# Due-time offsets for the engines' orders, and the down product's last chunk once a unit

## What is computed

```python
x = x + attn_a(layernorm(x))    # stage a: 8 heads of 64, low-rank keys and values, softmax over all 512
x = x + ffn(layernorm(x))       # stage f, two layers deep
x = x + attn_b(layernorm(x))    # stage b: 16 heads of 16, causal, score = dot^2 / (|q|^2 + |k|^2 - 2 dot + eps)
x = x + ffn(layernorm(x))       # stage f again, the same weights

def _layer(x, ...):             # one of the two layers of ffn
    q, k, v = split(shift_token(x) @ wqkv)          # 8 heads of 64, l2norm, rotary
    x = x + local_attention(q, k, v) @ wo           # window of 128 and the one before it
    h = layernorm(shift_token(x)) * lg + lb
    a, g = split(h @ w1 + b1)                       # 2 x 682 hidden features
    return x + (a * gelu(g)) @ w2 + b2              # the down product: 682 -> 256
```

## Time and profile before

| | us |
|---|---|
| median of 3 runs | 4440.92 |
| lowest, highest | 4433.65, 4452.77 |
| the profiled execution | 4441.2 |
| its span, first to last instruction | 4439.1 |
| TensorE busy with matmuls | 4132.5 (93%) |
| VectorE busy | 3291.9 (74%) |
| ScalarE busy | 2541.6 (57%) |
| GpSimd busy | 1674.8 (38%) |

### The profile page before, as it was taken

The page is one execution under the profiler, slowest core; times in us unless marked ns, Lnnn a source line. Parts: engine busy times, 40 slices in busy tenths (PEclk is TensorE's granted clock), DMA queues, the critical chain, the costliest instruction groups (busy, mean ns, idle before and its releaser), DMA issues.

```text
span 4439.1 us, 65596 instructions
## 1 busy us (share of the span) xinstructions
PE 4132.5 (93%) x23120; PEld 2596.3 (58%) x23120; DVE 3291.9 (74%) x7689; ACT 2541.6 (57%) x5480; POOL 1674.8 (38%) x1816
## 2 busy tenths in 40 slices
PE   8999989999999999987888877888999999999997
PEld 4665556666666666655555555555566666666664
DVE  5667677777767766659899999988677776677663
ACT  4555554445445445439888998876444454454441
POOL 2222355545545555430001001013565464465541
PEclk9999999999999999998889998988999999999998
DMA  2000000000001000000000001101000000100000
GB/s 79 10 16 6 24 11 6 3 3 4 24 8 30 15 8 8 26 19 20 20 21 22 22 18 28 37 18 34 3 6 3 3 25 8 32 17 17 13 20 22
DMA packets 63093, 78.57 MB, mean 18 GB/s; under 512 B 15344, under 2 KB 47392, under 8 KB 62768
## 3 DMA queue, kind: packets, MB, share of 16 engines
q1 hardware_dynamic: 62768, 74.39, 6.0%
HBM read 36.63 MB, written 12.58 MB: 11 GB/s over the span
## 4 chain that ended last, share of the span: by engine, by line
PE 65%; DVE 21%; issue 6%; ACT 5%; POOL 2%; DMA 0%; SPq 0%; POOLq 0%; DVEq 0%; ACTq 0%
PE wide L865 45%; PE o_ps L865 8%; PE wide L868 6%; PE turn_ps L868 5%; DVE x L1287 2%; DVE w_up L1387 2%; DVE turned L1338 2%; DVE prob L1399 1%; DVE w_up L1381 1%; DVE x L1393 1%; PE turn_ps L865 1%; DVE prob L1410 1%; POOL prob L1602 1%; ACT prob L1243 1%; DVE hid L1393 1%
## 5 line engine op out<-in xcount | busy, mean ns | idle before, releaser
L865 PE MATMUL wide<-x,w_up 128*128 128x512 f32 (+3 forms) x2528 | 843.0, 545 | 4.2 <-DVE x L1490 2.4
L865 PE MATMUL wide<-w_in,x_t 128*128 128x512 f32 (+2 forms) x1920 | 813.4, 568 | 17.5 <-ACT q_t L1164 8.1
L1602 POOL TENSOR_SCALAR prob<-prob,st 128x256 f32<-128x256 f32 (+1 forms) x1024 | 501.5, 508 | 758.8 <-DVE st L1423 756.4
L1223 ACT ACTIVATE prob<-prob,st 128x256 f32<-128x256 f32 (+1 forms) x1024 | 479.2, 471 | 259.9 <-DVE st L1410 259.5
L865 PEld LDWEIGHTS wide<-w_in,x_t 128*128 128x128 f32 x1920 | 342.2, 192 | 369.4 <-issue 360.6
L865 PEld LDWEIGHTS wide<-x,w_up 128*128 128x128 f32 (+2 forms) x2528 | 371.5, 195 | 289.5 <-issue 275.8
L865 PE MATMUL o_ps<-pt,v 128*32 128x128 f32 (+2 forms) x5120 | 500.0, 340 | 20.5 <-DVE pt L1439 9.9
L1575 POOL TENSOR_TENSOR sines<-raw,rot 128x512 f32<-128x512 f32 x256 | 354.0, 1403 | 331.2 <-ACT raw L1152 331.1
L1583 POOL TENSOR_TENSOR rn<-ss,minus_half 128x16 f32<-128x16 f32 x128 | 423.8, 3311 | 105.5 <-DVE ss L1333 98.7
L865 PEld LDWEIGHTS o_ps<-pt,v 128*64 128x64 f32 (+1 forms) x5120 | 322.1, 131 | 234.3 <-issue 145.6
L1254 ACT ACTIVATE o_t<-o_ps 128x512 f32<-128x512 f32 x192 | 114.2, 595 | 493.3 <-PE o_ps L865 493.3
(11 more groups left out here) (161 smaller groups left out, 7472.7 us busy)
## 6 DMA issues: line engine op xcount, KB each, us to landing
kept<-resid SPq DMA_DIRECT2D x16, 512.0 KB, 2.9
x<-kept SPq DMA_DIRECT2D x16, 512.0 KB, 3.3
w_up<-hid SPq DMA_DIRECT2D x62, 128.0 KB, 2.2
x<-hid SPq DMA_DIRECT2D x62, 128.0 KB, 2.4
shifted<-resid SPq DMA_DIRECT2D x32, 224.0 KB
w_in<-in_f_wqkv SPq DMA_DIRECT2D x4, 1536.0 KB, 6.5
w_up<-in_f_w SPq DMA_DIRECT2D x4, 1492.0 KB, 6.4
resid<-in_x SPq DMA_DIRECT2D x8, 512.0 KB, 8.9
```

The source lines that it names most:

```text
L865: return eng.matmul(out, lhsT, rhs, start=start, stop=stop, skip_group_check=True)
L1223: last = eng.activation(pr[:, local_span(t)], pr[:, local_span(t)], ACT.Exp, bias=sm[:, t:t + 1], scale=-1.0, accum_out=sm[:, 4 + t:5 + t])
L1602: last = eng.tensor_scalar(pr[:, local_span(t)], pr[:, local_span(t)], sm[:, 8 + t:9 + t], 1.0, ALU.mult, ALU.mult)
```

## The change

It has four pieces. `put` adds an offset from a new table, `DUE`, to a part's due time, by stage and kind; the table has 49 entries, for each of the three stages, between -0.284 and +0.31 units. `PATIENCE` goes from 0.3 to 0.321. The planned costs of the four `down` parts go from 2.3, 2.9, 2.3, 2.9 to 2.3, 2.3, 2.3, 3.4. And the 42-row products of all four tiles are issued behind the last tile's large ones, where they stood two by two behind the second and the fourth; since groups of two tiles in one bank are then open together, only tiles 0 and 2 start theirs with the start flag.

```diff
@@ cost
     if kind == "down":
-        return 2.9 if i % 2 else 2.3
+        return 3.4 if i == TILES - 1 else 2.3
@@ new
+DUE = {
+    ("f", "ss"): 0.022, ("f", "exp"): -0.039, ("f", "xt"): 0.015, ("f", "proj"): -0.076, ("f", "pt_a"): 0.074, ("f", "wt"): 0.161,
+    ("f", "raw"): 0.001, ("f", "pt_b"): -0.215, ("f", "rn"): -0.052, ("f", "nrm_h"): 0.11, ("f", "up_h"): -0.159, ("f", "inv"): 0.138,
+    ("f", "spread"): 0.092, ("f", "qk"): -0.021, ("f", "xt_c"): 0.102, ("f", "cos"): 0.073, ("f", "bn_f"): -0.014, ("f", "mix"): -0.114,
+    ("f", "res2"): 0.019, ("f", "join"): 0.004, ("f", "v_c"): -0.076,
+    ("a", "inv"): 0.001, ("a", "nrm_h"): -0.112, ("a", "ak_c"): -0.027, ("a", "pt_a"): 0.005, ("a", "aq"): 0.049, ("a", "mix"): 0.129,
+    ("a", "exp"): 0.061, ("a", "low"): 0.009, ("a", "xt_c"): 0.035,
+    ("b", "olog"): -0.057, ("b", "bqkv"): 0.046, ("b", "dup_b"): -0.232, ("b", "bn_h"): 0.31, ("b", "xt_c"): -0.017, ("b", "dup_a"): -0.272,
+    ("b", "bnum"): -0.044, ("b", "xt"): 0.053, ("b", "sel"): -0.065, ("b", "res"): -0.132, ("b", "brow"): -0.027, ("b", "turn_b"): -0.027,
+    ("b", "bclose"): -0.004, ("b", "bsq"): -0.284, ("b", "bss"): -0.066, ("b", "mix"): 0.123, ("b", "row"): -0.118, ("b", "bq"): 0.021,
+    ("b", "bden"): -0.001,
+}
@@ parts_of
     def put(kind, i, due, *follows):
-        out.append((kind, i, due, [f for f in follows if f is not None]))
+        out.append((kind, i, due + DUE.get((st, kind), 0.0), [f for f in follows if f is not None]))
@@ ordered
-PATIENCE = 0.3
+PATIENCE = 0.321
@@ the down product in tensor_program
                     for m in range(HC - 1):
-                        last = mm(ps[:, t * DIM:(t + 1) * DIM], hid[:, m, t * P:(t + 1) * P], w_down[:, m, :], m == 0, False)
-                    if i % 2:
-                        for t in DOWN_TILES[i - 1:i + 1]:
+                        last = mm(ps[:, t * DIM:(t + 1) * DIM], hid[:, m, t * P:(t + 1) * P], w_down[:, m, :], m == 0 and t % 2 == 0, False)
+                    if i == TILES - 1:
+                        for t in DOWN_TILES:
                             last = mm(ps[:, t * DIM:(t + 1) * DIM], hid[LAST_ROWS[t // 2], HC - 1, t * P:(t + 1) * P],
                                       w_down[LAST_ROWS[t // 2], HC - 1, :], False, True)
```

## The result

The changed kernel is slower. Its median is 4491.7 us (4 runs, 4485.9 to 4492.8), that of the kernel before beside it 4437.9 (4 runs, 4433.7 to 4452.8); the ratio is 1.0107, with a 95% interval of 1.008 to 1.0135. I had forecast 4402 and a range up to 4452. One execution of the kernel of experiment 9 took 4959.4 us at a granted clock of 0.84 and is left out of its ratio.

What follows compares the result with a forecast made beforehand. TensorE was taken to bound the feed-forward work and VectorE stage b. From 4441 us, 10.9 for the merged small products and 28 for the new order came off: 4402 us, range 4362 to 4452.

Steps and rivals of the forecast that it cites:

- Part 1: Down product: one block of small products per unit instead of two saves 0.35 us a unit, 10.9 us in all.
- part 2: The offsets and wider window change the engines' orders: 28 us gained, 16 at three edges and 12 in b.
- zero on the steady parts: Steady feed-forward units: the new order gains nothing, with under 0.6 us of 84 not busy on TensorE.
- only 6 us could be had there: Stage a: TensorE's idle time of 6.0 us, counted in the 108.9 us ceiling outside b.
- 6 us for changes of mode: Steady feed-forward units: one half-row block meeting more or less, about 0.2 us a unit, 6 us either way, range only.
- My own test in the last part: Steady feed-forward units: a change of over 1 us would mean the method was wrong about changes between full and half rows.
- minus 12 us: Stage b: the new order gives back a seventh of VectorE's 82.7 us idle time, 12 us.
- The third rival: Stage b: late clipping starves VectorE, 0.3 us a step over 192 steps, 58 us, so 4488 us; chance 0.12.
- the slack of 1.0 us a step: Stage b: the pair products' slack, TensorE's idle 197.6 us over 192 steps; delay beyond it makes VectorE wait.

Runs made afterwards that it cites:

- experiment 9: The changed kernel with added TensorE products in b, two ahead of pair products and two ahead of the transposes' wait: 4469.6 us, ratio 1.0031 to the kernel before.
- experiment 4: The kernel before with only the -0.004 offset of the closing product in b, small down products unmerged: 4469.5 us, ratio 1.0054.
- experiment 6: The merge of the small down products plus f's -0.021 offset for the query and key product, against the merge alone: 4459.3 us in one run.

## Why the prediction was wrong

**Part 1 was right.** 0.35 us a unit by the timeline was 0.36 in the profile, the eight small products took the 1.15 us worked out, and steady f units came to 83.4, where I had forecast 83.3, but only in the merge alone. The rule that a packed group costs one matmul and a few ns (the Trainium skill, "TensorE: Matmul & The Clock Gate", Measured speedup vs the span model) would have had no gain. The 0.36 us sides with the Trainium skill's page that has a change of mode drain the engine ("TensorEngine Tiling (Array Packing)", Key Properties).

**The step that failed is the sum for part 2.** I took TensorE's and VectorE's idle time as a ceiling, a share of it as the gain (28 us), and put zero on the steady parts, since a unit there is nearly all busy. Measured, part 2 was worth +62 us: the 51 between the spans and the 11 of the merge (by the table: -21 for a and the edge behind it, +36.5 and the merge's 11 for f, +35 for b). It has three terms, and I had the sign wrong in two and the place wrong in the third:

- *a*: the earlier trace rows show TensorE busy 434.0 of 440 us, so I wrote that only 6 us could be had there. The offsets took 2.1 us off each unit of 67, some 13 us over those 440 (an estimate, 6.5 units), twice that bound. A busy TensorE was not a full one: a transpose is shown as some 0.28 us long while the next starts 0.11 us after it, so gaps of up to some 0.16 us behind each group never appear as idle (an estimate, the difference of the two). In a steady unit of a, 396 matmuls before and after, the idle time shown fell from 1.0 to 0.35 us, a third of the 2.1. The count of matmuls in a stretch (2581, then 2632) shows what the busy share hides.
- *f*: zero, with 6 us for changes of mode. It was +1.5 us in each steady unit beside the merge's -0.35. A ceiling on gains says nothing on a loss, and in a it was no ceiling either. My own test in the last part (over 1 us in a steady unit) fired, though the cause was not the changes of mode that I named but one exposed wait of 1.65 us.
- *b*: minus 12 us, measured +35.

**The third rival had the start of the mechanism right, with too low a chance.** I named the broken tie between closing product and clipping, the later release of the wide place, and the slack of 1.0 us a step, and priced it at 58 us; experiment 4 has 24 us by the ratio and 31.8 over all eight units of b. That its 4488 us lies 4 us from the measured time is luck: b lost 35 us, not 58, and f's loss and a's gain, which it did not have, make up the rest. Its end was wrong as well: I expected VectorE to wait for the pair products, and it waits 0.8 us for them in two units, the rest for other work that TensorE and ScalarE bring late. I gave it 0.12, because VectorE's waits of the earlier trace rows were short. That was evidence on the old order alone. A tie that an offset of any size breaks is a repeated edit (the closing product is first in 171 places instead of 45, not always as I wrote), and should have been counted as the surest part of the change, not as a mishap. Its price has, on the likeliest reading of experiment 9, a second part that the prediction left out, the clock: the row of PEclk at 0.87 to 0.92 in b showed that TensorE was already at the lower of its two levels (1.2 GHz) for part of the time.

**The planner.** Its own account had the changed order 3 us shorter in all, f 1.2 us a unit longer, a 2.5 a unit shorter and b 1.3 a unit shorter. The chip has +1.2, -2.1 and +9. It was right on a and on this order of f, wrong on b, where the lower clock isn't in its costs, and wrong in size on the offset of experiment 6.

## What to carry to other kernels

Idle time in a trace bounds neither what an order can take nor, where matmuls overlap, what it can give back: price each order edit from both sides, and look first for ties, since an offset of any size decides them all. When a step frees a scarce buffer for the bounding pair of engines, keep it ahead of work of equal rank. Judge offsets stage by stage (a's set gained, f's and b's lost), because one sum hides three answers, and count instructions per us rather than busy time where matmuls overlap.

## What was unexpected of the hardware

**The same order takes different times in b.** Before, merge alone and merge with a's offsets have one order there. Two windows of about a unit each, the kernel before and then merge with a's offsets:

```profile
2408.00:2538.00 130.00, 105.60 (x863) 68.49 (x864) 125.61 (x263) 116.97 (x208) 12.20 (x18) 0.92 0.09 21
2538.00:2668.00 130.00, 105.59 (x866) 68.53 (x862) 125.61 (x265) 116.96 (x208) 12.21 (x18) 0.92 0.08 21
```

```profile
2390.00:2526.00 136.00, 113.89 (x854) 72.46 (x848) 125.34 (x260) 116.47 (x208) 12.21 (x18) 0.85 0.08 20
2526.00:2663.00 137.00, 114.89 (x864) 73.14 (x864) 125.81 (x261) 117.45 (x210) 12.21 (x18) 0.85 0.08 20
```

Same matmuls, same VectorE, 129.7 against 136.5 us a unit, and in each execution the length repeats for three units. What differs is the granted clock, 0.92 against 0.85, that is some 20 and 41 us of the unit at 1.2 GHz. All else in TensorE's queue is alike; ahead of a fall it did what it does all through b, products with waits of 0.6 to 3.4 us between them. The 17 us between 962.3 and 979.5 are as large as many a change. The record of the kernel before bears this out: in the 74 executions that ran beside the experiments, 4425 to 4471 us long, the mean granted clock went from 0.966 to 0.947, and time and clock go together closely (correlation -0.95), some 23 us for each 0.01. Which of the two drives the other they can't tell. If the clock does, the changed kernel's 0.950 to 0.953, against a median of 0.959 before, would be 14 to 21 us of its loss, an estimate by that slope. Why adding work in this order lifts the clock but not the speed, while in the changed order it does both, stays open.
